# An attention loop's rounded copies of q and k: made by VectorE behind each pair's second reciprocal instead of by ScalarE

## The chip, the cores and the metric

One core of one Trainium2 chip runs the whole program in one launch. The metric is the device time of that launch in microseconds (us); lower is better.

## What is computed

The reference is a two-layer block over 16 sequences of 256 tokens with 256 features: a gated folding layer, then an attention layer with a mixture of eight experts behind it. The change is in the attention:

```python
h = _ln(x, ln1_g, ln1_b) + shift
qkv = (h @ Wqkv.T).reshape(b, n, 3, H, HD)               # H = 16 heads of HD = 64
q = _ln(qkv[:, :, 0].transpose(0, 2, 1, 3), qn_g, qn_b)
k = _ln(qkv[:, :, 1].transpose(0, 2, 1, 3), kn_g, kn_b)
scores = jnp.einsum('bhnd,bhmd->bhnm', q, k) / jnp.sqrt(jnp.float32(HD))
attn = jax.nn.softmax(scores, axis=-1)
o = jnp.einsum('bhnm,bhmd->bhnd', attn, v)
```

Matrix products that need float32 accuracy are made of three products of rounded parts. An operand `x` is split into `x_h`, its value rounded to the matmul's fp32r type, and `x_l = x - x_h`; the product is `x_h*y_h + x_h*y_l + x_l*y_h`.

## The kernel before

`attention` runs a software pipeline over batches. Step `t` works on eight pairs of heads, `s` = 0 to 7, of batch `t`, while it prepares batches `t+1` to `t+3` and finishes `t-1`. Each engine has its own instruction list, written out by hand in program order; semaphores tie them together. An engine that waits holds up all that stands behind in its list.

In one pair, TensorE makes the scores of two heads (L1107), then transposes the probabilities of the pair before (L1119), then does filling work: transposes of prepared q and k (`fill`, L1200), blocks of the qkv projection (`chunk`, with L147 as the line of its matmuls), the output projection, and in every second pair the products with v (L1134). The softmax of the pair goes VectorE `lowest_of` (L1493, row minima), ScalarE `exps` (L1262), VectorE `invert` (L1499, one reciprocal for each head, sides 0 and 1), GpSimd `divide` (L1392, one for each head), and back to TensorE's transposes in the next pair.

Beside this the q and k of batch `t+1` are prepared in eight blocks j of 128 x 512. A chunk of the projection lands in one of two PSUM banks. ScalarE copies it out (L1306) and squares it into `raw_sq` (L1308); only then is the bank free for the next chunk but one. VectorE sums the squares (`total`, L1489). ScalarE's square of chunk e waits for the sum of chunk e-2, because there are two `raw_sq` buffers:

```python
wait(act, summed, 8, b, e - 1)
nc.scalar.activation(raw_sq[e % 2][:, :], chunk_bank[j % 2][:, :], ACT.Square).then_inc(chunk_out, 1)
```

TensorE waits for that bank in `chunk` with `wait(pe, chunk_out, 12, b, j - 1)`. GpSimd scales the block (`norm`, L1380), TensorE transposes it (L1200), ScalarE puts the affine part on it (`empty`, L1286, which also frees the one transpose bank), ScalarE makes the rounded high part (`high_parts`, L1321), and GpSimd makes the low part (`low_parts`, L1386). In the first step, `t` = -1, VectorE makes the low parts (L1553). The places in the lists are:

```python
HIGH_PAIR = [3, 4, 5, 5, 6, 6, 7, 7]
LOW_PLACE = [(3,1),(4,1),(5,1),(5,1),(6,1),(6,1),(7,1),(7,1)]
CHUNK_PAIRS = [6, 6, 7, 7, 0, 0, 1, 1, 4, 4, 5, 5]
```

So the pairs 5, 6 and 7 hold two high parts each, and 3 and 4 hold one. GpSimd's list in such a pair is: divide side 0, divide side 1, low parts. In pair 5 a low part of the layer's input (`a_l`, L1418) stands between them; it waits for VectorE's `a_h` (L1547). In pair 6 the tiny power op for `rstd` (L1406) stands ahead of the divides, and VectorE's two normalizing ops (L1462) wait for it. VectorE's list in pair 7 is: the minima, `o_l` (L1512), reciprocal 0, the copy of `pT` (L1524), two statistics, a total, reciprocal 1 (L1499), two aggregates (L1475), the variance `out_var` (L1478, 128 x 2 elements), the second total (L1489), and then the minima of the next step's pair 0 (L1493). Step 14 is a little different: block 7 is emptied late in pair 7, and its high part stands behind that.

Of the kernel before, what the change touches and what calls it, by code (L numbers as in the profile page):

```python
# [20 lines left out]
ACT = mybir.ActivationFunctionType  # L21
# [3 lines left out]
NB, T, D = 16, 256, 256  # L25
# [15 lines left out]
def live(b):  # L41

    return not isinstance(b, int) or 0 <= b < NB


def wait(eng, sem, per, b, n):


    if n <= 0:
        b, n = b - 1, n + per  # L50
    if live(b):
        eng.wait_ge(sem, b * per + n)
# [814 lines left out]
HIGH_PAIR = [3, 4, 5, 5, 6, 6, 7, 7]  # L867
# [56 lines left out]
def fill_at(t, i):  # L924

    if i < 0:
        t, i = t - 1, i + 2 * PAIRS
    for name, j, slot in TR_FILLS:
        if slot == LATE_FILL and t == LAST_NEAR[0]:
            slot += 1  # L930
        if slot == i:
            return t + TR_LAG[name], name, j
    return -1, None, 0


def attention(nc, exponent, weights, rows_of, banks, ident, x1_rows, hbias, cols, x2_rows, logit, out, a, halves, sbuf, sems):
# [3 lines left out]
    x1_in, spread_in, spread_out, normed_x, tr_h, out_h, a_hi, a_lo, x1_out = norm_sems  # L940
    s = ExitStack()
    with s:
# [11 lines left out]
        qT_h, qT_l, kT_h, kT_l = (sbuf(s, n, [P, 12, T], F32R) for n in ("qT_h", "qT_l", "kT_h", "kT_l"))  # L954
# [31 lines left out]
        def closing(b):  # L986

            return isinstance(b, int) and b == NB - 1
# [19 lines left out]
        def o_part(o, q, its, n):  # L1008

            return o[:, o_at(q, its):o_at(q, its) + n, :].rearrange("p k t -> p (k t)")  # L1010
# [8 lines left out]
        def block_of(parts, j, its):  # L1019

            e = QK_ORDER[j]
            part = parts[e % QKC // 2]
            at = 4 + 4 * its if e % 2 else 0
            return part[:, at:at + 4, e // QKC * P:(e // QKC + 1) * P]

        def raw_block(j):

            return raw[:, QK_ORDER[j], :].rearrange("p (m n) -> p m n", m=4)
# [23 lines left out]
        with nc.Block() as block:  # L1052
# [202 lines left out]
            def _(act):  # L1255
# [17 lines left out]
                def empty(b, name, j, its):  # L1273
                    if name is None or not live(b) or name == "h" and first(b):
                        return
                    if name == "h":
                        wait(act, tr_h, 1, b, 1)
                        wait(act, a_lo, 1, b - 1, 1)
                        for k in range(KT):
                            last = nc.scalar.activation(aT[:, k, :], tr[:, k * T:(k + 1) * T], ACT.Identity,  # L1280
                                                        bias=hbias[:, k, bass.ds(b, 1)], scale=cols[:, LN1_G + k:LN1_G + k + 1])
                        last.then_inc(out_h, 1)
                    if name == "qk":
                        wait(act, tr_qk, 8, b, j + 1)
                        g = QN_G if QK_ORDER[j] % QKC < 2 else KN_G
                        nc.scalar.activation(raw_block(j), tr[:, :].rearrange("p (m n) -> p m n", m=4), ACT.Identity,  # L1286
                                             bias=cols[:, g + 1:g + 2], scale=cols[:, g:g + 1]).then_inc(out_qk, 1)
                    if name == "x2":
                        wait(act, tr_x2, 1, b, 1)
                        nc.scalar.activation(x2T[:, :, :].rearrange("p k n -> p (k n)"), fill_bank(b)[:, :], ACT.Copy).then_inc(out_x2, 1)  # L1290
                    if name == "gates":
                        wait(act, tr_gates, 1, b, 1)
                        nc.scalar.activation(logit[:, bass.ds(b * TT, TT), :], fill_bank(b)[:, 0:TT * E].rearrange("p (n e) -> p n e", n=TT), ACT.Copy).then_inc(out_gates, 1)

                def projected(b, n):
                    wait(act, tr_proj, TT, b, n + 1)
                    wait(act, tr_gates, 1, b - 1, 1)
                    nc.scalar.activation(proj[:, n, :], proj_bank(b, n)[:, 0:D], ACT.Copy).then_inc(out_proj, 1)
# [13 lines left out]
                            act.wait_ge(wo_lo, FIRST_LO + 4)  # L1312
                        nc.scalar.activation(v[1 - odd][:, n, (c - QKC) * 512:(c - QKC + 1) * 512], chunk_bank[j % 2][:, :], ACT.Copy).then_inc(chunk_out, 1)

                def high_parts(t, s, js, odd):
                    for j in js:
                        if live(t + 1) and HIGH_PAIR[j] == s:
                            if t == -1 and j == 0:
                                act.wait_ge(x1_out, 16 * NB)
                            wait(act, out_qk, 8, t + 1, j + 1)  # L1320
                            nc.scalar.activation(block_of((qT_h, kT_h), j, 1 - odd), raw_block(j), ACT.Copy).then_inc(qk_hi, 1)  # L1321

                def step(t, odd):
                    for s in range(PAIRS):
                        if not closing(t) and not closing(t - 1):
                            if s - 1 in PROJ_PAIRS and live(t - 1):
                                projected(t - 1, PROJ_PAIRS.index(s - 1))
                            empty(*fill_at(t, 2 * s - 1), 1 - odd)
                        for b, q, its, n in taken_at(t, s, odd):
                            if live(b):  # L1330
                                wait(act, pv_done, PAIRS, b, q + n)
                                if q in (0, 2):
                                    wait(act, tr_proj, TT, b - (2 if q == 0 else 1), TT)
                                nc.scalar.activation(o_part(o_h, q, its, n), result_of(b, q, n), ACT.Copy).then_inc(o_hi, n)
                        if closing(t) or closing(t - 1):
                            empty(*fill_at(t, 2 * s - 1), 1 - odd)
                        for n in range(TT):
                            if live(t + 1) and s == SEED_PAIR[n]:
                                seeds(t + 1, n)
                        late = t == LAST_NEAR[0] and s == PAIRS - 1  # L1340
                        if live(t):
                            exps(t, s, (0,))
                        if not late:
                            empty(*fill_at(t, 2 * s), 1 - odd)
                        if live(t):
                            exps(t, s, (1,))
                        b, q, _ = pair_at(t, s, 1, odd)
                        if live(b):
                            wait(act, pT_done, H, b, 2 * q + 1)
                            wait(act, pv_done, PAIRS, b, q - 1)  # L1350
                            nc.scalar.activation(pT[q % 2 * 2][:, :, :].rearrange("p m n -> p (m n)"), pT_bank[0][:, :], ACT.Copy).then_inc(pT_act, 1)  # L1351
                        high_parts(t, s, range(7 if late else 8), odd)
                        if late:
                            empty(*fill_at(t, 2 * s), 1 - odd)
                            high_parts(t, s, (7,), odd)
                        for c, j in chunks_at(t, s):
                            if live(c):
                                chunk(c, j, odd)
                        if closing(t) and s in PROJ_PAIRS:
                            projected(t - 1, PROJ_PAIRS.index(s))  # L1360
                        for q in range(4):
                            if t == -1 and s == WOUT_HIGH_PAIR[q]:
                                nc.scalar.activation(flat(wo_h[:, :, :])[:, q * 512:(q + 1) * 512], flat(o_raw)[:, q * 512:(q + 1) * 512], ACT.Copy).then_inc(wo_hi, 1)
                        if live(t) and s == PIECE_PAIRS[0]:
                            wait(act, ew_piece, 32, t, 16)
                            wait(act, ew_stored, 32, t - 1, 32)
                            nc.scalar.activation(ew_h[:, :], ew_raw[:, :], ACT.Copy).then_inc(ew_piece, 8)
# [57 lines left out]
            def _(dve):  # L1425
# [69 lines left out]
                def invert(t, s, side):  # L1495
                    at = s % 2 * 2 + side
                    wait(dve, exped, H, t, 2 * s + side + 1)
                    wait(dve, shared, H, t, 2 * s + side - 3)
                    nc.vector.reciprocal(share[:, at, :], denom[:, at, :]).then_inc(inverted, 1)  # L1499

                def step(t, odd):
                    far = t + 2
                    for s in range(PAIRS):
# [29 lines left out]
                            link.settle()  # L1533
                        if live(t):
                            invert(t, s, 1)
                        if s == OUT_STATS_PAIR:
                            for part in range(TT + 1, 2 * TT + 2):
                                out_norm(t, s, part)
# [600 lines left out]
```

## Time and profile before

| | |
|---|---|
| median of 3 runs | 1431.31 us (1430.86 to 1431.76) |
| the profiled execution | 1430.09 us, of which the span is 1428.3 us |
| busy: PE, ACT, DVE, POOL | 96%, 73%, 67%, 64% of the span |
| mean granted TensorE clock | 0.987 |

The profile has a page of the whole run, groups of instructions by line, waits, a timeline of single instructions for any stretch and busy time by window. PE is TensorE, ACT ScalarE, DVE VectorE, POOL GpSimd. A time such as 663.20 is us from the start of the span. The steps of the attention loop lie between about 326 and 1155 us, and the steps 2 to 13 repeat each other with a period of 50.8 us. Most rows below are from the end of step 5 and the start of step 6, whose pair 0 begins at 662.80.

### The profile page before, as it was taken

How to read it: one execution, taken by the hardware profiler on the slowest of the kernel's cores; microseconds unless marked ns; L12 is line 12 of the kernel's file. 1: busy time of each engine (PE TensorE's matmuls, PEld its weight loads, DVE VectorE, ACT ScalarE, POOL GpSimd, SP SyncE). 2: the span in 40 equal slices, each digit the busy share in tenths (PEclk: the TensorE clock that was granted, in tenths of full speed). 3: DMA queues.
4: the chain of work that ended last, by engine and by line, in shares of the span. 5: the costliest groups of instructions: out<-in, count | busy, mean ns of one | idle time of the engine just before them, and what ended most of it. 6: DMA issues, size and time to landing. Idle time of an engine off the chain costs nothing. (4 is left out here: it accounts for less than half of the span.)

```text
span 1428.3 us, 30431 instructions
## 1 busy us (share of the span) xinstructions
PE 1370.0 (96%) x10795; PEld 1184.1 (83%) x10795; DVE 960.9 (67%) x2191; ACT 1035.7 (73%) x2703; POOL 912.5 (64%) x855
## 2 busy tenths in 40 slices
PE   7899999997999999999999999999999988999996
PEld 6799999996688887887888888788888678889896
DVE  6876677654776676676667667667756568678763
ACT  5566666565898889889889888988988732476662
POOL 2576666652678768867877876886777620354643
PEclk9899999999999999999999999999999999999999
DMA  5342222110100100110110010011011046145522
GB/s 159 122 122 67 68 68 69 50 51 23 38 9 31 53 23 31 53 45 9 53 46 31 31 53 28 26 53 45 9 45 46 31 143 258 45 104 155 138 34 30
DMA packets 61638, 89.04 MB, mean 62 GB/s; under 512 B 6144, under 2 KB 50992, under 8 KB 58800
## 3 DMA queue, kind: packets, MB, share of 16 engines
q1 hardware_dynamic: 53232, 75.82, 16.4%
q0 software_dynamic: 6144, 8.39, 3.6%
q10 hardware_dynamic: 2112, 2.88, 0.6%
q8 instruction: 87, 1.43, 0.4%
q14 instruction: 63, 0.52, 0.1%
HBM read 61.90 MB, written 25.18 MB: 61 GB/s over the span
## 5 line engine op out<-in xcount | busy, mean ns | idle before, releaser
L1392 POOL TENSOR_TENSOR prob<-prob,share_p 128x512 f32<-128x512 f32 x256 | 271.6, 1067 | 196.1 <-DVE share_p L1499 195.6
L1493 DVE TENSOR_REDUCE shift<-bank 128x2 f32<-128x512 f32 x256 | 164.7, 685 | 185.9 <-PE bank L1107 185.8
L1262 ACT ACTIVATE prob<-bank,shift 128x256 f32<-128x256 f32 x512 | 237.8, 479 | 63.9 <-DVE shift L1493 63.8
L147 PE MATMUL bank<-wqkv_h,rowsT_h 128*128 128x512 f32 x384 | 159.3, 415 | 2.0 <-PEq L311 1.7
L147 PE MATMUL bank<-wqkv_h,rowsT_l 128*128 128x512 f32 x384 | 151.7, 395 | 0.0
L147 PE MATMUL bank<-wqkv_l,rowsT_h 128*128 128x512 f32 x384 | 151.3, 394 | 0.0
L1119 PE MATMUL bank<-ident,prob 128*128 128x128 f32 x1024 | 143.0, 281 | 1.3 <-POOL prob L1392 1.3
L1380 POOL TENSOR_TENSOR landing<-landing,rq 128x512 f32<-128x512 f32 x128 | 131.1, 1046 | 10.1 <-DVE rq L1447 10.1
L1134 PE MATMUL bank<-pT,landing 128*64 128x256 f32 x1024 | 126.2, 386 | 1.7 <-ACT pT L1351 1.7
L1119 PEld LDWEIGHTS bank<-ident,prob 128*128 128x128 f32 x1024 | 109.6, 141 | 21.7 <-POOL prob L1392 4.2
L1262 ACT ACTIVATION_READ_ACCUMULATOR prob<-bank,shift 128x1 f32 x512 | 107.3, 210 | 0.0
L1286 ACT ACTIVATE landing<-bank,cols 128x512 f32<-128x512 f32 x128 | 101.9, 796 | 5.8 <-PE bank L1200 4.2
L644 POOL TENSOR_TENSOR hid_l<-hid,hid_h 128x512 fp32r<-128x512 f32 x64 | 86.3, 1358 | 30.6 <-ACT hid_h L540 29.9
L536 ACT ACTIVATE hid<-bank,cols 128x256 f32<-128x256 f32 x128 | 53.3, 470 | 68.1 <-PE bank L147 67.9
L1134 PEld LDWEIGHTS bank<-pT,landing 128*64 128x64 f32 x1024 | 67.3, 137 | 40.8 <-issue 9.2
L1107 PE MATMUL bank<-kT_h,qT_h 64*128 64x256 f32 x512 | 85.6, 330 | 3.1 <-ACT prob L1262 3.1
L1489 DVE TENSOR_REDUCE ssq<-raw_sq 128x8 f32<-128x512 f32 x128 | 85.8, 672 | 3.2 <-ACT raw_sq L1308 2.6
L1524 DVE COPY pT<-bank 128x512 f32<-128x512 f32 x128 | 87.1, 681 | 0.4 <-PE bank L1119 0.4
L1306 ACT ACTIVATE landing<-bank 128x512 f32<-128x512 f32 x128 | 80.0, 625 | 9.1 <-PE bank L147 9.0
L1200 PE MATMUL bank<-ident,landing 128*128 128x128 f32 x512 | 78.4, 276 | 8.2 <-ACT landing L1286 3.7
L147 PEld LDWEIGHTS bank<-wqkv_h,rowsT_h 128*128 128x128 f32 x384 | 73.2, 191 | 15.5 <-issue 2.4
L147 PEld LDWEIGHTS bank<-wqkv_h,rowsT_l 128*128 128x128 f32 x384 | 72.7, 189 | 15.7
(324 smaller groups left out, 4518.3 us busy)
## 6 DMA issues: line engine op xcount, KB each, us to landing
landing<-in_fc1s SPq DMA_DIRECT2D x6, 1024.0 KB, 4.9
landing<-in_fc2s SPq DMA_DIRECT2D x6, 1024.0 KB, 5.1
rows<-in_x SPq DMA_DIRECT2D x16, 256.0 KB, 2.9
xT<-in_xT SPq DMA_DIRECT2D x16, 256.0 KB, 2.7
x_again<-in_x SPq DMA_DIRECT2D x16, 256.0 KB, 2.8
x_rows<-x SPq DMA_DIRECT2D x16, 256.0 KB, 3.2
rows<-x_rows SPq DMA_DIRECT2D x16, 256.0 KB, 3.1
x<-x_rows SPq DMA_DIRECT2D x16, 256.0 KB, 2.9
```

What stands on the lines that cost most here:

```text
L147: last = nc.tensor.matmul(out, a, b, start=(n == 0), stop=(n == 3 * len(ks) - 1))
L644: nc.gpsimd.tensor_tensor(hid_l[:, 2 * g:2 * g + 2, :], hid[:, 2 * g:2 * g + 2, :], hid_h[:, 2 * g:2 * g + 2, :].bitcast(F32), ALU.subtrac ...
L1107: mm = nc.tensor.matmul(score_bank[side][:, n * T:(n + 1) * T], q[r, at, n * P:(n + 1) * P], k[r, at, :], start=(i == 0), stop=(i == 2))
L1119: last = nc.tensor.transpose(pT_bank[side][:, m * T + n * P:m * T + (n + 1) * P], prob[q % 2 * 2 + side][:, n, m * P:(m + 1) * P], ident[: ...
L1134: last = nc.tensor.matmul(values_bank(b, q)[side * HD:(side + 1) * HD, :], v[its][:, m, h * HD:(h + 1) * HD], pT[q % 2 * 2 + side][:, m, : ...
L1262: last = nc.scalar.activation(prob[at][:, n, :], score_bank[side][:, n * T:(n + 1) * T], ACT.Exp, bias=shift[:, at, n:n + 1], scale=-1.0, ...
L1286: nc.scalar.activation(raw_block(j), tr[:, :].rearrange("p (m n) -> p m n", m=4), ACT.Identity, bias=cols[:, g + 1:g + 2], scale=cols[:, g ...
L1380: nc.gpsimd.tensor_tensor(part, part, rq[:, n, c * 8:(c + 1) * 8].unsqueeze(2).to_broadcast([P, 8, HD]), ALU.mult).then_inc(normed, 1)
L1392: nc.gpsimd.tensor_tensor(prob[at][:, :, :], prob[at][:, :, :], share[:, at, :].unsqueeze(2).to_broadcast([P, TT, T]), ALU.mult).then_inc( ...
L1489: nc.vector.tensor_reduce(ssq[:, n, c * 8:(c + 1) * 8], raw_sq[c % 2][:, :].rearrange("p (h d) -> p h d", h=8), AX, ALU.add).then_inc(summ ...
L1493: nc.vector.tensor_reduce(shift[:, s % 2 * 2 + side, :], score_bank[side][:, :].rearrange("p (n m) -> p n m", n=TT), AX, ALU.min).then_inc ...
L1524: nc.vector.tensor_copy(pT[q % 2 * 2 + 1][:, :, :].rearrange("p m n -> p (m n)"), pT_bank[1][:, :]).then_inc(pT_dve, 1)
```

## The change

The eight high parts of a step leave ScalarE's list. VectorE makes them with `tensor_copy`, in the same pairs, directly behind reciprocal 1 of the pair and ahead of whatever stood there. The semaphore `qk_hi` that the low parts wait for now counts VectorE's copies. Nothing else is moved.

```diff
 # scalar
-                def high_parts(t, s, js, odd):
-                    for j in js:
-                        if live(t + 1) and HIGH_PAIR[j] == s:
-                            if t == -1 and j == 0:
-                                act.wait_ge(x1_out, 16 * NB)
-                            wait(act, out_qk, 8, t + 1, j + 1)
-                            nc.scalar.activation(block_of((qT_h, kT_h), j, 1 - odd), raw_block(j), ACT.Copy).then_inc(qk_hi, 1)
...
-                        high_parts(t, s, range(7 if late else 8), odd)
                         if late:
                             empty(*fill_at(t, 2 * s), 1 - odd)
-                            high_parts(t, s, (7,), odd)
...
 # vector
+                def high_parts(t, s, odd):
+                    for j in range(8):
+                        if live(t + 1) and HIGH_PAIR[j] == s:
+                            if t == -1 and j == 0:
+                                dve.wait_ge(x1_out, 16 * NB)
+                            wait(dve, out_qk, 8, t + 1, j + 1)
+                            nc.vector.tensor_copy(block_of((qT_h, kT_h), j, 1 - odd), raw_block(j)).then_inc(qk_hi, 1)
...
                         if live(t):
                             invert(t, s, 1)
+                        high_parts(t, s, odd)
                         if s == OUT_STATS_PAIR:
                             for part in range(TT + 1, 2 * TT + 2):
                                 out_norm(t, s, part)
```

## Rows read from the trace of the kernel before

**Rows 1.** The page: the span, and each engine's busy time.

```profile
span 1428.3 us, 30431 instructions
PE 1370.0 (96%) x10795; PEld 1184.1 (83%) x10795; DVE 960.9 (67%) x2191; ACT 1035.7 (73%) x2703; POOL 912.5 (64%) x855
```

**Rows 2.** Windows, one steady step: length, then busy time and count by engine.

```profile
561.20:612.00 50.80, 50.70 (x394) 41.52 (x394) 34.56 (x77) 44.43 (x124) 38.73 (x36) 1.00 0.12 38
```

**Rows 3.** One line's instructions, L1321: ns min/median/max, first and last start.

```profile
L1321 ACT ACTIVATE qT_h<-landing x64: 612/648/657, 342.4 to 1117.0; 128x512 fp32r<-128x512 f32 x64
```

**Rows 4.** The same for the lines L1547 and L1478 of DVE.

```profile
L1547 DVE CAST rowsT_h<-rowsT x15: 414/415/643, 355.6 to 1056.3; 128x512 fp32r<-128x512 f32 x15
...
L1478 DVE TENSOR_SCALAR out_var<-out_moment x16: 168/962/968, 460.1 to 1163.6; 128x2 f32<-128x2 f32 x16
```

**Rows 5.** Timeline, DVE, end of pair 7: start, us, instruction, [idle before].

```profile
662.97 0.15 DVE L1499 RECIPROCAL share_p<-denom 128x2 f32<-128x2 f32 x1
663.04 0.23 DVE L1475 BATCH_NORM_AGGREGATE out_moment<-out_stats 128x2 f32<-128x6 f32 x2
663.30 0.96 DVE L1478 TENSOR_SCALAR out_var<-out_moment 128x2 f32<-128x2 f32 x1
664.18 0.67 DVE L1489 TENSOR_REDUCE ssq<-raw_sq 128x8 f32<-128x512 f32 x1
664.77 1.27 DVE L1493 TENSOR_REDUCE shift<-bank 128x2 f32<-128x512 f32 x2
```

**Rows 6.** Timeline, POOL, the same stretch.

```profile
663.20 1.04 POOL L1392 TENSOR_TENSOR prob<-prob,share_p 128x512 f32<-128x512 f32 x1 [1.00 <-DVE share_p L1499]
664.20 1.29 POOL L1386 TENSOR_TENSOR qT_l<-landing,qT_h 128x512 fp32r<-128x512 f32 x1
```

**Rows 7.** Timeline, ACT, the same stretch: the square of chunk e = 3.

```profile
664.89 0.60 ACT L1308 ACTIVATE raw_sq<-bank 128x512 f32<-128x512 f32 x1
```

**Rows 8.** Timeline, PE: first matmul of pair 0's second chunk.

```profile
666.16 0.39 PE L147 MATMUL bank<-wqkv_h,rowsT_h 128*128 128x512 f32 x1
```

**Rows 9.** Timeline, DVE and POOL, two casts elsewhere that meet POOL.

```profile
55.81 1.42 DVE L703 CAST rowsT_h<-rowsT 128x512 fp32r<-128x512 f32 x1
...
304.71 0.43 DVE L703 CAST h_h<-hT 128x512 fp32r<-128x512 f32 x1
...
55.67 1.28 POOL L689 TENSOR_TENSOR xT_l<-xT,xT_h 128x512 fp32r<-128x512 f32 x1
56.90 1.48 POOL L644 TENSOR_TENSOR hid_l<-hid,hid_h 128x512 fp32r<-128x512 f32 x1
...
304.77 1.51 POOL L672 TENSOR_TENSOR x_b<-x_again,ffn_b 128x512 f32<-128x512 f32 x1
```

**Rows 10.** Timeline, ACT from pair 5 to 6, and PE's fill of pair 6.

```profile
649.49 1.17 ACT L1321 ACTIVATE kT_h<-landing 128x512 fp32r<-128x512 f32 x2
...
651.48 0.82 ACT L1286 ACTIVATE landing<-bank,cols 128x512 f32<-128x512 f32 x1
...
651.86 0.49 PE L1119 MATMUL bank<-ident,prob 128*128 128x128 f32 x3
652.45 0.30 PE L1200 MATMUL bank<-ident,landing 128*128 128x128 f32 x1
```

**Rows 11.** Timeline, DVE and POOL, pair 6 and the start of 7.

```profile
655.40 2.17 DVE L1462 TENSOR_SCALAR rows<-rows,moment,rstd 128x256 f32<-128x256 f32 x2 [0.40 <-POOL rstd L1406]
659.12 0.69 DVE L1493 TENSOR_REDUCE shift<-bank 128x2 f32<-128x512 f32 x1 [1.55 <-PE bank L1107]
...
655.33 2.09 POOL L1392 TENSOR_TENSOR prob<-prob,share_p 128x512 f32<-128x512 f32 x2
```

**Rows 12.** Timeline, step 15: DVE's minima of pair 0, PE's scores of pair 1.

```profile
1118.42 1.28 DVE L1493 TENSOR_REDUCE shift<-bank 128x2 f32<-128x512 f32 x2
...
1121.11 0.39 PE L1107 MATMUL bank<-kT_h,qT_h 64*128 64x256 f32 x2 [0.32 <-ACT prob L1262]
```

**Rows 13.** Timeline, DVE, the first minima of step 0.

```profile
365.04 1.28 DVE L1493 TENSOR_REDUCE shift<-bank 128x2 f32<-128x512 f32 x2
```

## The prediction

> **What bounds the kernel now.** I read the page first, then one steady step by windows, then single instructions on all four engines around the places of the change. The page shows TensorE (PE) busy for 96% of the span, ScalarE 73%, VectorE 67% [rows 1]. One steady step shows it more sharply: PE is busy 50.70 of 50.80 us, ScalarE 44.43, VectorE 34.56 [rows 2]. So ScalarE has 6 us to spare per step and VectorE 16 us; neither sum sets the time. What ScalarE gives back is worth only what PE waits for it, and what VectorE gets costs nothing unless it makes a PE instruction late. The question is therefore one of order: which PE instruction stands close behind the places where VectorE now does more.
>
> **What is removed from ScalarE.** Per step eight activations of 0.65 us [rows 3], 5.2 us, 16 times over. Where does PE wait for ScalarE? In a steady step I find one place. In pair 5 two high parts run from 649.49 for 1.17 us, the chunk copies follow, then the `empty` that frees the transpose bank, 651.48 to 652.30. PE's next fill starts at 652.45, so 0.15 us is the delay from a ScalarE end to a PE start. The last of the three transposes ahead of it starts at about 652.08 (0.11 us between such starts), so the fill begins 0.37 us behind it where 0.11 would do [rows 10]. Without the two high parts `empty` is ready well before; the gain is 0.26 us per step. I count 13 steps: -3.4 us.
>
> **What VectorE gets.** Eight copies of 128 x 512. The same form, `a_h`, takes 0.415 us at the median (0.414 to 0.643) [rows 4]: 3.3 us per step, which the 16 us would hold. But these copies do not run alone. `out_var` on 128 x 2 elements takes 0.168 us at its shortest and 0.962 at the median [rows 4]. In the timeline it starts at 663.30, just behind POOL's divide (663.20, 1.04 us), and ends at 664.26, with the divide [rows 5, 6]. It was blocked for the whole POOL instruction. A cast elsewhere does the same: issued 0.14 us behind a POOL start it takes 1.42 us and ends 0.28 us behind POOL's end (57.23 against 56.95), and the next POOL instruction takes 1.48 us where its neighbour takes 1.28. A cast issued 0.06 us ahead of a POOL start keeps its 0.43 us and POOL takes 1.51, 0.23 longer, which is the 0.37 us of overlap less 0.14 [rows 9].
>
> The Trainium skill has a rule for this (SBUF — State Buffer, Who interferes with whom): a VectorE instruction that uses both of its SBUF ports, as fp32 copies and scalar ops between SBUF tensors do, and a GpSimd instruction exclude each other, and the one that issues first holds the pair to its end. The rows agree on the blocking (0.962 against 0.168 us); the skill gives no price for the 0.20 us of the next GpSimd instruction. By the rule the copies are the wrong work to put just where GpSimd's divide starts. Without the rule the sum would be -3.4 us.
>
> **Pair 7, step by step.** Reciprocal 1 starts at 662.97 and the next VectorE instruction at 663.04; the divide it releases starts at 663.20 [rows 5, 6]. So:
> - Cast of block 6: starts 663.05, 0.15 ahead of the divide, wins, ends 663.47. The divide loses 0.27 - 0.14 = 0.13 and ends at 664.37 instead of 664.24.
> - Cast of block 7: issued 663.39 with the divide under way, blocked, ends 664.37 + 0.28 = 664.65.
> - POOL's low part of block 6 needs only the first cast. It starts at 664.33 and takes 1.29 [rows 6] + 0.20 = 1.49, to 665.82.
> - The two aggregates follow the second cast by the old distances, and `out_var` is issued at 664.83, 0.26 behind the first aggregate [rows 5]. POOL is again busy: it ends at 665.83.
> - The second total started at 664.18, now 665.75: 1.57 us late. ScalarE's square of chunk 3 started 0.71 behind that total's start (664.89) and took 0.60 [rows 7]: now 666.46 to 667.06.
> - PE's second chunk of pair 0 needs that bank. It started at 666.16 [rows 8]; the bank was free at 665.49, with 0.15 of delay 665.64, so the slack is 0.52. Now the earliest start is 667.06 + 0.15 = 667.21: PE waits 1.05 us.
>
> The minima of pair 0 come 1.57 us late as well (664.77 before [rows 5]), and with them exps, reciprocals and divides. Pair 0 has room for that: the next scores move back by the same 1.05 us. I count nothing more. This holds for steps 1 to 13, which have both `out_var` and a chunk 3: 13 x 1.05 = +13.7 us.
>
> **The other pairs.** In pairs 3 and 4 one cast is added; pair 3's moves the weight-piece subtraction behind the divide, pair 4's waits for a divide. Both find PE busy with chunks or the projection. In pair 5 the two casts make `a_h`, and behind it `a_l` and two low parts, some 0.8 us late; their readers are in a later pair. In pair 6 the two casts come ahead of the two normalizing ops, which today take 2.17 us because each waits out a divide [rows 11]. VectorE then has four such instructions in a row, each let in at the end of one POOL instruction (a low part, the power op, two divides). The divides move back about 1.1 us, so they end near 658.6 and VectorE is free at 658.7. The minima of pair 7 are due at 659.12, or 658.86 if the 0.26 of pair 6 is gained, and VectorE idles 1.55 us ahead of them today [rows 11]. It fits, barely: cost nothing. If it does not, what is late next is the whole of pair 7.
>
> **The ends.** Step 14 has no chunk 3, but its pair 7 holds both casts and `out_var`. By the same working the minima of step 15 come about 1.6 us late (1118.42 before), and PE's scores of pair 1, which already waited 0.32 us for exps [rows 12], come 1.6 us late: +1.6. In step -1 VectorE now makes high and low parts in turn, so the first minima (365.04 [rows 13]) come some 0.5 us late and the scores of the next pair follow; against it I put 0.2 for ScalarE's relief there: +0.3.
>
> **Sum.** -3.4 + 13.7 + 1.6 + 0.3 = +12.2 us. Against the profiled execution (1430.09 us, span 1428.3) that is 1442.3; the median of the runs is 1.2 us above that execution, so 1431.31 + 12.2 = 1443.5 us. The cost is borne by one wait. If each of its parts is off by 0.3 us (the boundary of one POOL instruction is a step, not a slope), it is 13 x 0.3 = 4 us either way.
>
> **Rivals.**
> - *The POOL conflict costs PE nothing (faster).* The copies take 0.42 us each at plain price, in time that `out_var` spends waiting today (0.96 against 0.17 us). For it: VectorE has 16 us of room per step. The point that decides is the second total of pair 7: if it is late by less than 0.52 us, PE's chunk starts on time and only ScalarE's relief is left: -3.4 us, 1428 us. Against it: `out_var` would have to get in ahead of the low part, and [rows 9] show that a waiting cast takes that opening.
> - *Both casts get in ahead of the divide (slower, less).* The second is issued 0.08 us before the first one's end. Then the divide ends about 0.5 us late, PE's transposes of pair 7 wait for it, and `out_var` waits for the divide alone; the total is 0.6 late, about the slack. Per step +0.5 - 0.26, and +1 at the ends: +4, 1435 us. Against it: in [rows 9] a POOL instruction that is waiting starts as the blocker ends.
> - *Pair 6 overruns (slower, more).* If the last normalizing op misses the second divide's end, it waits for a low part of 1.29 us [rows 6], the minima of pair 7 are about 0.8 us late, and all of pair 7's chain with them: 13 x 0.8 = 10 more, 1453 us.
> - *Nothing to be seen (same).* The relief and a small stall balance: within 3 us.
>
> **Chances.** Forecast 0.62; the first rival 0.08; both casts ahead 0.11; pair 6 overruns 0.12; balance 0.07. About 0.2% (2.9 us) is what a measurement of this kernel can tell from no change. Slower 0.85, same 0.08, faster 0.07. The range takes in the smaller-loss rival and nearly the overrun: 1435 to 1452; the forecast's own is 1439 to 1448.
>
> **What would show it.** In the changed profile: no ScalarE copies of q and k; in pairs 5 to 7 one cast near 0.42 us and one near 1.3; `out_var` starting more than 1 us later and still near 1 us long; ScalarE's square of chunk 3 waiting about 1.5 us for the total; a PE wait of about 1 us in L147 for that square, once a step; a period of 51.6 us in place of 50.8; the 0.37 us ahead of pair 6's fill gone. A period of 50.5 would make the first rival right; a late first minimum in pair 7 the third.

## The result and the profile after

The changed kernel took 1446.58 us (median of 4 runs, 1445.95 to 1451.81) where the kernel before took 1431.53 us beside it. The ratio is 1.0116, with a 95% interval of 1.0102 to 1.0130: slower by 1.2%. The medians differ by 15.0 us; the forecast was +12.2 us and the range 1435 to 1452.

The profiled execution is the slowest of the four, 1451.81 us. Up to PE's scores of step 15, pair 1 (1137.85, against 1121.11 in [rows 12]) it is 16.74 us behind the one before. The other 5.0 us come after that, where the records of granted clock show two half-clock stretches of 10.2 us (from 1139.4 and 1183.8) and before one of 3.4 us (from 1165.9). The other three runs are 5 to 6 us shorter at a granted clock of 0.988 to 0.989 (0.982 here), so I count those 5.0 us to that execution and not to the change.

Page: the span and each engine's busy time.

```profile
span 1450.0 us, 30432 instructions
PE 1381.2 (95%) x10795; PEld 1188.1 (82%) x10795; DVE 1046.5 (72%) x2319; ACT 974.2 (67%) x2575; POOL 926.6 (64%) x855
```

Exactly 128 instructions went from ACT to DVE; DVE's busy time rose by 85.6 us, ACT's fell by 61.5 [rows 1]. 128 plain casts of 0.415 us are 53 us: the other 32 us are, by the rows below, instructions that are counted as busy while they are blocked.

Windows, one steady step from pair 0 to pair 0, to be set beside [rows 2]: length, busy time and count of PE, PEld, DVE, ACT and POOL, then clock, DMA share and GB/s.

```profile
615.46:667.46 52.00, 51.09 (x394) 41.47 (x393) 39.79 (x85) 40.59 (x115) 39.61 (x36) 1.00 0.11 37
```

The period is 52.00 us in place of 50.77 to 50.81, and PE now has 0.91 us of idle time in it, where it had 0.10, with the same 394 matmuls to do. Its busy time is 0.39 us longer all the same, so part of what it loses stands as busy time in this view. What it waits for is in the view of waits (total us, times, longest); the first row below was not there before, and the second stood at 0.3 us once.

```profile
PE bank L147 <- ACT raw_sq L1308: 8.2, 13, 0.6
...
PE bank L147 <- issue: 3.8, 14, 0.5
```

The first is the wait that was forecast, 13 times. The view has only the 0.62 us between the modelled end of one matmul and the start of the next; the pair is 1.03 us longer. Timeline of pair 7's end (pair 0 of step 6 begins at 667.46), DVE, then POOL, ACT and PE; the rows answer to [rows 5 to 8].

```profile
667.62 0.15 DVE L1489 RECIPROCAL share_p<-denom 128x2 f32<-128x2 f32 x1
667.70 0.41 DVE L1497 CAST qT_h<-landing 128x512 fp32r<-128x512 f32 x1
668.02 1.26 DVE L1497 CAST kT_h<-landing 128x512 fp32r<-128x512 f32 x1
669.20 0.23 DVE L1465 BATCH_NORM_AGGREGATE out_moment<-out_stats 128x2 f32<-128x6 f32 x2
669.47 0.98 DVE L1468 TENSOR_SCALAR out_var<-out_moment 128x2 f32<-128x2 f32 x1
670.37 0.67 DVE L1479 TENSOR_REDUCE ssq<-raw_sq 128x8 f32<-128x512 f32 x1
...
667.86 1.14 POOL L1382 TENSOR_TENSOR prob<-prob,share_p 128x512 f32<-128x512 f32 x1 [1.01 <-DVE share_p L1489]
668.96 1.47 POOL L1376 TENSOR_TENSOR qT_l<-landing,qT_h 128x512 fp32r<-128x512 f32 x1
...
671.08 0.60 ACT L1308 ACTIVATE raw_sq<-bank 128x512 f32<-128x512 f32 x1 [2.25 <-DVE ssq L1479]
...
670.70 0.40 PE L147 MATMUL bank<-wqkv_h,rowsT_l 128*128 128x512 f32 x1
671.73 0.50 PE L147 MATMUL bank<-wqkv_h,rowsT_h 128*128 128x512 f32 x1 [0.62 <-ACT raw_sq L1308]
```

Read it downwards. The divide starts at 667.86, 0.16 behind the first cast, and ends at 669.00. The second cast, free to go at 668.02, ends at 669.28, 0.28 behind the divide. By then the low part is running (668.96 to 670.43), and `out_var`, 128 x 2 elements, stands for 0.98 us until that too is over. So the second total starts 2.91 us behind the start of pair 0, where it stood at 1.38 [rows 5]; the square of chunk 3 ends at 671.68 and PE's chunk starts 0.05 behind that end, 4.27 us behind the start of pair 0 in place of 3.36 [rows 8]. Pair 0 is 8.16 us long in place of 7.13.

The second wait, "issue", is not in the forecast. Timeline of pair 5's end and pair 6's start (654.84), DVE, POOL and PE.

```profile
653.71 0.17 DVE L1489 RECIPROCAL share_p<-denom 128x2 f32<-128x2 f32 x1 [0.20 <-DVE stats L1442]
653.79 1.59 DVE L1497 CAST kT_h<-landing 128x512 fp32r<-128x512 f32 x2
...
655.65 0.43 DVE L1546 CAST rowsT_h<-rowsT 128x512 fp32r<-128x512 f32 x1
...
656.16 1.26 POOL L1408 TENSOR_TENSOR rowsT_l<-rowsT,rowsT_h 128x512 fp32r<-128x512 f32 x1 [1.06 <-DVE rowsT_h L1546]
...
656.67 0.60 PE L1200 MATMUL bank<-ident,landing 128*128 128x128 f32 x4
657.52 0.47 PE L147 MATMUL bank<-wqkv_h,rowsT_h 128*128 128x512 f32 x1 [0.25 <-issue]
```

The fill (656.67) now follows the transposes without a gap, as forecast. But `a_h` is made behind the two casts, `a_l` (named `rowsT_l` here) ends at 657.42, and PE's next chunk starts 0.10 behind it. The code says why:

```python
if j == 0:
    wait(pe, a_hi, 1, b, 1)
    wait(pe, a_lo, 1, b, 1)
```

Chunk 0 stands in pair 6. Before, `a_l` ended 1.87 us behind pair 6's start and the chunk began 2.48 behind it; now these are 2.58 and 2.68. Pair 6 is 7.92 us long, where it was 7.72 to 7.76 and should have become 7.5.

### The profile page after: what moved, and what is told of

Read it like the earlier page. It is cut to its first block and busy times, and to the rows that moved or that the text cites. A ratio compares the mean times of both kernels' runs of the same rounds, so it can differ in the third digit from the quotient of the medians.

```text
span 1450.0 us, 30432 instructions
## 1 busy us (share of the span) xinstructions
PE 1381.2 (95%) x10795; PEld 1188.1 (82%) x10795; DVE 1046.5 (72%) x2319; ACT 974.2 (67%) x2575; POOL 926.6 (64%) x855
## 5 line engine op out<-in xcount | busy, mean ns | idle before, releaser
L147 PE MATMUL bank<-wqkv_h,rowsT_h 128*128 128x512 f32 x384 | 160.3, 417 | 13.7 <-ACT raw_sq L1308 8.2
L147 PE MATMUL bank<-wqkv_h,rowsT_l 128*128 128x512 f32 x384 | 151.9, 396 | 0.0
L147 PE MATMUL bank<-wqkv_l,rowsT_h 128*128 128x512 f32 x384 | 151.2, 394 | 0.0
L1308 ACT ACTIVATE raw_sq<-bank 128x512 f32<-128x512 f32 x128 | 80.3, 627 | 34.6 <-DVE ssq L1479 34.6
L147 PEld LDWEIGHTS bank<-wqkv_h,rowsT_h 128*128 128x128 f32 x384 | 72.8, 190 | 34.9 <-ACT raw_sq L1308 14.3
L1376 POOL TENSOR_TENSOR qT_l<-landing,qT_h 128x512 fp32r<-128x512 f32 x60 | 86.9, 1448 | 0.0
```

The source lines that it names most:

```text
L147: last = nc.tensor.matmul(out, a, b, start=(n == 0), stop=(n == 3 * len(ks) - 1))
L1376: nc.gpsimd.tensor_tensor(block_of((qT_l, kT_l), j, 1 - odd), raw_block(j), block_of((qT_h, kT_h), j, 1 - odd).bitcast(F32), ALU.subtract) ...
```

## The experiments

All of them are timed against the kernel before, in two groups: total_first to behind_a_h (median of before 1432.27 us) and pair5_only to reduce_copy (1430.56). The ratio is the one on record for runs taken side by side, not the quotient of the two medians. "Pair 0", "pair 6" and "pair 7" are the times from one pair's scores to the next pair's in a steady step.

| run | median us | ratio (95%) | period | pair 0 | pair 6 | pair 7 |
|---|---|---|---|---|---|---|
| before (profile) | 1431.53 | 1 | 50.8 | 7.13 | 7.72 | 4.70 |
| after (profile) | 1446.58 | 1.0116 (1.0102 to 1.0130) | 52.0 | 8.16 | 7.92 | 4.69 |
| total_first | 1435.07 | 1.0026 (1.0016 to 1.0037) | 51.1 | 7.23 | 7.94 | 4.70 |
| tiny_copies | 1427.84 | 0.9972 (0.9959 to 0.9984) | 50.55 | 7.16 | 7.47 | 4.70 |
| pair7_only | 1448.85 | 1.0108 (1.0091 to 1.0125) | 52.0 | 8.16 | 7.92 | 4.69 |
| behind_a_h | 1464.94 | 1.0227 (1.0210 to 1.0244) | 53.35 | 9.04 | 7.47 | 5.61 |
| pair5_only | 1440.40 | 1.0073 (1.0059 to 1.0086) | 51.5 | 8.01 | 7.47 | 4.82 |
| end_of_pair | 1426.64 | 0.9971 (0.9961 to 0.9981) | 50.5 | 7.13 | 7.47 | 4.70 |
| block7_tiny | 1443.77 | 1.0093 (1.0078 to 1.0109) | 51.9 | 7.98 | 7.95 | 4.70 |
| reduce_copy | 1439.79 | 1.0069 (1.0053 to 1.0085) | 51.4 | 7.88 | 7.62 | 4.70 |

**1. The second total ahead of `out_var`.** If PE waits for the square because `out_var` holds the total up, changing their order takes the wait away and leaves both casts where they are.

```diff
                         if s == OUT_STATS_PAIR:
-                            for part in range(TT + 1, 2 * TT + 2):
+                            for part in range(TT + 1, 2 * TT + 1):
                                 out_norm(t, s, part)
...
                         if before:
                             total(*before[1])
+                        if s == OUT_STATS_PAIR:
+                            out_norm(t, s, 2 * TT + 1)
```

> The changed kernel with one thing reordered on VectorE in pair 7: out_var stands behind the second total instead of ahead of it; both casts stay behind reciprocal 1. Theory (the loss of pair 0 comes from out_var waiting out a GpSimd low part with the total behind it): the total is late by the two casts and one divide only, about 0.6 us, against a slack of 0.5, so PE's wait for the square of chunk 3 shrinks from 1.04 to about 0.1 us a step; 13 steps give about -12 us against the changed kernel, +4 to +5 us (+0.3%) against the kernel before. Rival (VectorE is simply late by the casts' own time, wherever out_var stands): no more than 0.2 us a step comes back, +13 us or more against the kernel before.

The ratio fell from 1.0116 to 1.0026, and the wait for `raw_sq` left the list of waits. Its timeline, DVE and ACT (pair 0 begins at 663.10):

```profile
663.65 1.26 DVE L1497 CAST kT_h<-landing 128x512 fp32r<-128x512 f32 x1
...
665.00 0.65 DVE L1479 TENSOR_REDUCE ssq<-raw_sq 128x8 f32<-128x512 f32 x1
665.57 0.52 DVE L1468 TENSOR_SCALAR out_var<-out_moment 128x2 f32<-128x2 f32 x1
...
665.68 0.60 ACT L1308 ACTIVATE raw_sq<-bank 128x512 f32<-128x512 f32 x1 [1.22 <-DVE ssq L1479]
```

The second cast is as long as before, 1.26 us, yet the total comes 1.90 us behind pair 0's start in place of 2.91. The two casts alone make it 0.52 late (1.38 before), which is the slack that the forecast gave the chunk. The 0.1 us that pair 0 still loses is not that wait: side 1's divide, 1.14 us in place of 1.04, brings the transposes of pair 7's side 1 0.10 us late (1.59 us behind pair 0's start in place of 1.49). The other microsecond is `out_var` behind the low part. Of the 0.3 us of period that are left, 0.2 are pair 6.

**2. Tiny copies.** The same instructions, on 2 of each head's 128 columns from step 1 on; most of the high parts is left out.

```diff
-nc.vector.tensor_copy(block_of((qT_h, kT_h), j, 1 - odd), raw_block(j)).then_inc(qk_hi, 1)
+n = P if t < 1 else 2
+nc.vector.tensor_copy(block_of((qT_h, kT_h), j, 1 - odd)[:, :, 0:n], raw_block(j)[:, :, 0:n]).then_inc(qk_hi, 1)
```

> The changed kernel, but from step 1 on each of VectorE's copies covers only 2 of every 128 columns (128 x 8 elements in place of 128 x 512), so the high parts are mostly stale there; instruction count and order are unchanged. Theory (blocking by the GpSimd instruction under way, not the copies' length): the second cast and out_var each still wait out a GpSimd instruction, the second total is still about 1.2 us late, PE still waits about 0.7 us a step, and the kernel stays some 8 us (+0.5%) above the kernel before. Rival (the copies' own 0.42 us each are the cost): the loss goes, and with ScalarE's relief the time is 3 us under the kernel before.

What I expected failed: nothing was blocked that had not been before. DVE, then POOL:

```profile
661.21 0.15 DVE L1498 CAST qT_h<-landing 128x8 fp32r<-128x8 f32 x1
661.27 0.17 DVE L1498 CAST kT_h<-landing 128x8 fp32r<-128x8 f32 x1
...
661.37 1.04 POOL L1382 TENSOR_TENSOR prob<-prob,share_p 128x512 f32<-128x512 f32 x1 [1.00 <-DVE share_p L1489]
```

Two such casts start 0.06 us apart and both start ahead of the divide. So this was no test of the blocking. It bounds the other side: with VectorE's part nearly free, the kernel is 0.28% faster (0.16 to 0.41%), which agrees with the -3.4 us (0.24%) of the forecast's first term for ScalarE's relief.

**3. Only block 7's copy tiny.** This leaves the first cast at full length, so that the second meets a divide under way (most of block 7's high part is left out).

```diff
+n = P if t < 1 or j < 7 else 2
```

> The changed kernel, but from step 1 on the copy of block 7 alone covers 2 of every 128 columns, so that block's high part is mostly stale; block 6 in front of it is copied in full, as are all others. This mends the run with all copies tiny, where both were through before the divide began. Theory (blocking): block 7's tiny copy is issued under the divide, waits it out and takes about 1.0 us in place of 0.15, out_var then waits out the low part, the second total is 1.3 to 1.4 us late and pair 0 still takes about 8.0 us: +13 to +15 us against the kernel before. Rival (the copies' length): 0.4 us of VectorE time are gone, the total is late by no more than block 6's 0.35 us, pair 0 takes 7.1 to 7.2 us, +3 us or less against the kernel before.

DVE, then POOL:

```profile
665.36 0.41 DVE L1498 CAST qT_h<-landing 128x512 fp32r<-128x512 f32 x1
665.68 1.00 DVE L1498 CAST kT_h<-landing 128x8 fp32r<-128x8 f32 x1
...
666.87 1.06 DVE L1468 TENSOR_SCALAR out_var<-out_moment 128x2 f32<-128x2 f32 x1
...
665.52 1.14 POOL L1382 TENSOR_TENSOR prob<-prob,share_p 128x512 f32<-128x512 f32 x1 [1.01 <-DVE share_p L1489]
666.62 1.28 POOL L1376 TENSOR_TENSOR qT_l<-landing,qT_h 128x512 fp32r<-128x512 f32 x1
```

A cast of 128 x 8 elements takes 1.00 us here and 0.17 us in experiment 2. It costs nearly what the full one does: pair 0 is 7.98 us, 0.85 of the 1.03 us lost, and the kernel 13.2 us slower, as expected. It is the place of the second copy that is paid for, its size hardly.

**4. The same copies by an operation that is not blocked.** `tensor_reduce` with the maximum over one element copies too.

```diff
-nc.vector.tensor_copy(block_of((qT_h, kT_h), j, 1 - odd), raw_block(j)).then_inc(qk_hi, 1)
+nc.vector.tensor_reduce(block_of((qT_h, kT_h), j, 1 - odd), raw_block(j).unsqueeze(3), AX, ALU.max).then_inc(qk_hi, 1)
```

> The changed kernel with each copy made by a tensor_reduce over one element (a maximum), at the same places; it takes about 0.67 us in place of 0.41, like the other reductions of this size, which were never seen to be blocked. Theory: neither copy is blocked and GpSimd is not slowed (its low parts back to 1.29 us), but out_var still falls behind the low part of block 6 and waits it out; the total is about 1.2 us late, pair 0 takes 7.8 us, pair 6 about 7.7: +8 to +11 us against the kernel before. Rival (the casts' own conflict with GpSimd is the whole of the loss): within 3 us of the kernel before.

DVE, then POOL:

```profile
666.03 0.68 DVE L1497 TENSOR_REDUCE kT_h<-landing 128x512 fp32r<-128x512 f32 x1
666.62 0.24 DVE L1465 BATCH_NORM_AGGREGATE out_moment<-out_stats 128x2 f32<-128x6 f32 x2
666.89 1.03 DVE L1468 TENSOR_SCALAR out_var<-out_moment 128x2 f32<-128x2 f32 x1
...
665.61 1.04 POOL L1382 TENSOR_TENSOR prob<-prob,share_p 128x512 f32<-128x512 f32 x1 [1.00 <-DVE share_p L1489]
666.60 1.29 POOL L1376 TENSOR_TENSOR qT_l<-landing,qT_h 128x512 fp32r<-128x512 f32 x1
```

The copy runs through under the divide in 0.68 us, and the divide and the low part keep their 1.04 and 1.29 us. The Trainium skill says the same of `tensor_reduce` (SBUF — State Buffer, Who interferes with whom): on trn2 it never contends with GpSimd; the trace agrees, 0.68 us beside a divide and 0.67 elsewhere. Yet the pair still loses 0.75 us: `out_var` (666.89) comes 0.29 us behind the start of the low part (666.60). So the loss needs no blocked cast; any delay that brings `out_var` behind that start is enough. It does not follow that blocking is harmless in the changed kernel. These copies start 0.59 us apart, where plain casts that find GpSimd idle start 0.33 apart (experiment 8). By that estimate two plain casts that were not blocked would put `out_var` at about 666.37, 0.23 ahead of the low part. No run here has such casts; if the estimate is right, it is the blocking of the second cast that makes the delay long enough.

**5. Part of the change: pair 7 alone.** Blocks 0 to 5 stay on ScalarE, 6 and 7 go to VectorE. So that `qk_hi` counts in order, each copy waits for the one before it.

```diff
+ON_ACT, ON_DVE = (0, 1, 2, 3, 4, 5), (6, 7)
...
 # scalar, in its old place
+wait(act, qk_hi, 8, t + 1, j)
...
 # vector, behind reciprocal 1
+wait(dve, qk_hi, 8, t + 1, j)
```

> The kernel before with only blocks 6 and 7 (pair 7) given to VectorE behind reciprocal 1; blocks 0 to 5 stay on ScalarE, with a wait that keeps the count of high parts in order. Theory (pair 7 alone carries the loss of pair 0): pair 0 takes 8.17 us in place of 7.13 as in the changed kernel, 13 x 1.04 = +13.5, and +2 at the two ends: about +15 us (+1.0 to +1.1%) against the kernel before, with pair 6 at its old 7.72. Rival (the loss needs the backlog of all pairs): +8 us or less.

Pair 0 is 8.16 us, exactly that of the full change: pair 7's two copies make the whole of this loss. Pair 6 did not keep its old 7.72. Timeline of ACT in pair 5:

```profile
654.57 1.39 ACT L1323 ACTIVATE kT_h<-landing 128x512 fp32r<-128x512 f32 x2
```

It is 0.22 us longer than the same two in [rows 10]: with the added wait the second no longer overlaps the first. The `empty` behind them, and with it the fill of pair 6, come about 0.2 us later. That is my edit and not the change, and the ratio of this run (1.0108) says nothing of pair 6.

**6. Pair 5's copies behind `a_h`.** If `a_l` is what holds the chunk of pair 6 up, this brings pair 6 down to 7.5.

```diff
-                        high_parts(t, s, odd)
+                        if s != SPLIT_PAIR:
+                            high_parts(t, s, odd)
...
                             nc.vector.tensor_copy(a_h[:, :, :], aT[:, :, :]).then_inc(a_hi, 1)
+                        if s == SPLIT_PAIR:
+                            high_parts(t, s, odd)
```

> The changed kernel with the two casts of pair 5 moved behind a_h. Theory (pair 6 lost 0.20 us instead of gaining 0.26 because a_h and with it GpSimd's a_l came late, and PE's first chunk of pair 6 waits for a_l): a_h is on time, pair 6 takes 7.46 in place of 7.92 us, and 12 steps give -5.5 us against the changed kernel, so about +11 us (+0.8%) against the kernel before; pair 0 keeps its 8.17. Rival (pair 6 is late for another reason, such as VectorE's late minima there): no change against the changed kernel, or slower, because the minima of pair 6 come still later.

Pair 6 came down to 7.47 us, and the waits of L147 put down to "issue" went with it. But the kernel is 2.3% slower than before, where 0.8% was expected. DVE, from pair 5 to pair 7, then PE:

```profile
660.63 1.83 DVE L1497 CAST kT_h<-landing 128x512 fp32r<-128x512 f32 x2
662.38 1.28 DVE L1483 TENSOR_REDUCE shift<-bank 128x2 f32<-128x512 f32 x2
...
665.81 0.99 DVE L1497 CAST qT_h<-landing 128x512 fp32r<-128x512 f32 x1
666.72 1.26 DVE L1497 CAST kT_h<-landing 128x512 fp32r<-128x512 f32 x1
667.90 2.67 DVE L1452 TENSOR_SCALAR rows<-rows,moment,rstd 128x256 f32<-128x256 f32 x2
670.49 1.28 DVE L1483 TENSOR_REDUCE shift<-bank 128x2 f32<-128x512 f32 x2
...
673.28 0.39 PE L1107 MATMUL bank<-kT_h,qT_h 64*128 64x256 f32 x2 [0.85 <-ACT prob L1262]
...
675.75 0.66 PE L1119 MATMUL bank<-ident,prob 128*128 128x128 f32 x4 [0.91 <-POOL prob L1382]
```

Now the minima of pair 6 are the late ones: 2.18 us behind its start, where they stood at 1.15 in the changed kernel. Its four blocked instructions then stand at 665.81 to 670.57, one POOL instruction after the other, and the minima of pair 7 follow at once (670.49). This is the overrun of the third rival. The changed kernel is clear of it by the 0.82 us that DVE idles ahead of those minima:

```profile
663.77 1.29 DVE L1483 TENSOR_REDUCE shift<-bank 128x2 f32<-128x512 f32 x2 [0.82 <-PE bank L1107]
```

A shift of about a microsecond uses them up, and pair 7 (5.61) and pair 0 (9.04) pay.

**7. Pair 5's copies alone, behind `a_h`,** the other six on ScalarE, with the same added wait as in experiment 5 (`ON_DVE = (2, 3)`).

> The kernel before with only blocks 2 and 3 (pair 5) given to VectorE, behind a_h; the other six stay on ScalarE, with waits that keep the count of high parts in order. Theory: ScalarE's relief in pair 5 ends PE's wait at pair 6's fill (7.46 to 7.50 us for pair 6 in place of 7.74), a_h is on time, and the late minima of pair 6 (about 1 us, as in the run with the casts behind a_h) cost nothing because VectorE has only the two normalizing ops to do in pair 6 and can catch up before pair 7: -2.5 to -3.5 us (-0.2%) against the kernel before. Rival: the late minima of pair 6 already make pair 7 late, and the time is 5 us or more above the kernel before.

The ratio is 1.0073: the rival's time came, but not by its way. ACT, then PE:

```profile
660.85 0.61 ACT L1309 ACTIVATE raw_sq<-bank 128x512 f32<-128x512 f32 x1
...
662.47 0.51 ACT L1263 ACTIVATE prob<-bank,shift 128x256 f32<-128x256 f32 x1
...
666.96 0.66 PE L1120 MATMUL bank<-ident,prob 128*128 128x128 f32 x4 [0.81 <-POOL prob L1394]
```

Pair 6 has its 7.47, but its minima start late. The minima of pair 7 are on time again (1.01 us behind its start, as before the change); it is ScalarE that does not catch up. It works without a gap from pair 6's exponentials to those of pair 7 (662.47), which start 2.70 us behind the pair's start in place of 1.74, and these and their divide are late for PE. The added wait on ScalarE can account for little of these 0.96 us directly: in pair 6 its two high parts start 0.75 us apart in place of 0.53.

**8. All copies at the end of their pair.** The same eight copies, placed behind everything else in VectorE's list for the pair: behind `out_var` and the totals, behind `a_h`, behind the normalizing ops.

```diff
-                        high_parts(t, s, odd)
                         if s == OUT_STATS_PAIR:
...
                             chains(t, i + 1, spot)
+                        high_parts(t, s, odd)
```

> The changed kernel with all eight copies on VectorE, but at the end of the pair's list: behind the second total, a_h and the two normalizing ops. Theory (place, not work, made the loss): in pair 7 the total is on time, so pair 0 is back at 7.13 to 7.2; in pair 6 the normalizing ops are not queued behind casts, and the casts end before pair 7's minima are due, because GpSimd stands idle until it gets block 4; in pair 5 a_h is on time. ScalarE's relief remains: period 50.5 in place of 50.8, -2 to -4 us against the kernel before (ratio 0.998). Rival (16 us of idle VectorE time cannot be used at all, since some minima come late wherever the casts stand): 5 us or more above the kernel before.

1426.64 us over 9 runs, ratio 0.9971 to before (0.9961 to 0.9981): a small gain, clear of the noise, and faster than both kernels. Windows of one step, then DVE and POOL at the end of pair 7 (pair 0 begins at 659.91):

```profile
609.36:659.91 50.55, 50.55 (x395) 41.55 (x394) 39.47 (x85) 40.40 (x115) 39.51 (x36) 1.00 0.12 38
```

```profile
660.40 0.96 DVE L1468 TENSOR_SCALAR out_var<-out_moment 128x2 f32<-128x2 f32 x1
661.28 0.68 DVE L1479 TENSOR_REDUCE ssq<-raw_sq 128x8 f32<-128x512 f32 x1
661.88 0.41 DVE L1497 CAST qT_h<-landing 128x512 fp32r<-128x512 f32 x1
662.21 0.42 DVE L1497 CAST kT_h<-landing 128x512 fp32r<-128x512 f32 x1
662.54 1.28 DVE L1483 TENSOR_REDUCE shift<-bank 128x2 f32<-128x512 f32 x2
...
662.37 1.41 POOL L1376 TENSOR_TENSOR qT_l<-landing,qT_h 128x512 fp32r<-128x512 f32 x1 [1.03 <-DVE qT_h L1497]
```

PE is busy for the whole step. `out_var` still waits out the divide, as it did before the change, and the total is in its old place (1.37 us behind pair 0's start). Now POOL waits for the cast, and so both casts find it idle and take 0.41 and 0.42 us. The low part starts 2.46 us behind pair 0's start, where it stood at 1.40 [rows 6], and nobody misses it. DVE works as much as in the changed kernel (39.47 against 39.79 us): the same work costs 1.45 us of period less by its place alone.

## Why the prediction was right, and where it was not

The direction, the place and the size of the main term held.

- **Pair 7.** Each of these steps came within 0.1 us of the working: first cast ahead of the divide by 0.16 (0.15 forecast), second cast 0.28 behind the divide's end, low part 1.47 (1.49), total 2.91 behind the start of pair 0 (2.95), pair 0 longer by 1.03 (1.05), in the 13 pairs that were counted: 13.4 us (13.7). The last step has some luck in it: PE's chunk began 0.05 us behind the square and not 0.15, so it is 0.91 us late and not 1.05; but its second matmul follows the first after 0.33 us where it was 0.23, and that makes most of the rest. Experiment 1 shows `out_var` behind the low part to be the cause; experiments 3 and 4 show that a tiny but blocked second copy, or two slower ones that are not blocked, lead there too. That a change of order at one POOL boundary decides ("a step, not a slope") fits experiments 1 and 3; the delay at which the step lies was not tried.
- **ScalarE's relief.** The gain of 0.26 us per step was real: pair 6 is 7.47 in experiments 2, 6, 7 and 8.
- **The step that failed** is in pair 5: "a_h, and behind it a_l and two low parts, some 0.8 us late; their readers are in a later pair". Its size was about right (0.7 us), but the first reader of `a_l` is chunk 0 in pair 6, the very next pair. It takes the 0.26 back and 0.2 more, 12 times in steps 1 to 12: +2.5 us. In step 13 nothing stands between the casts and `a_h`, `a_l` ends 2.19 us behind the start of pair 6, and a gain is left (7.52 against 7.74); step 14 makes no `a_l` and has one too (5.88 against 6.00): together -0.35. The first term of the sum was -3.4 us and came out at +2.2. Experiment 6 shows the cause.
- **The ends.** Step 15, pair 0 is 5.87 in place of 4.36: +1.5 (+1.6 forecast). The first scores come 0.5 late, as forecast. In step 15, pair 1, the profiles of experiments 1, 3, 4 and 6 have 3.99 us where it was 4.47; the changed kernel's profile has 6.06 there, in a half-clock stretch, and cannot show whether it gets that 0.5 back. Step 0 is 0.8 us shorter in the profile after, where 0.2 was put, but that is the clock's doing: in the profile before it has a half-clock stretch at 384.2, in pair 4 (9.87 us), and none after (8.24), which is -1.6. That stretch comes and goes between the runs (pair 4 is 9.75 in experiment 4's profile). The other pairs of step 0 are 0.8 us longer (pair 0 by 0.5, pair 6 by 0.2), so apart from the clock the start costs about 1.3 us where the forecast had 0.3.
- **Pair 6 overruns.** "It fits, barely" held for the changed kernel, with 0.82 us left, but 0.46 of that is the length that pair 6 has beyond its 7.46; without it some 0.36 would be left (an estimate), where the forecast had 0.16. Its four instructions were not all held up as forecast: the first cast takes 0.77 us and the second 0.41 (659.42 and 660.12), beside the power op. Experiment 6 shows how near the overrun was.

The sum of the profile up to step 15, pair 1: 13.4 + 2.2 + 1.5 + 0.5 - 0.8 = 16.8 us, which are the 16.74 us by which it is behind. This is one profile cut into its parts and not a second measurement. The medians differ by 1.7 us less, and by 3.4 us less once the half-clock stretch of step 0 is taken out; that rest is not explained. The median came out 3.1 us above the forecast, and the 5.6 us by which pair 6 missed its term are more than that.

The rivals: no cost to PE, both casts ahead of the divide, and balance are ruled out by the rows of pair 7; the overrun did not come in this kernel.

## What to carry to other kernels

When a copy moves to VectorE, ask in which gap of GpSimd's list it falls, not only how long it takes. Here the same eight copies cost 15 us directly behind the instruction that releases GpSimd, and gained 4 behind VectorE's own urgent work, with GpSimd waiting for the copy. Moving only pair 5's two to a later place, behind `a_h`, made it worse: a loss of 33 us. The price is not paid by the copy alone but by the next short instruction that slips past the start of the following GpSimd instruction, and by whatever waits for that one. And of everything that stands behind a new instruction, look up the first reader in the code, in each list; "in a later pair" was true of `a_l` here, but the later pair was the next one, and that step cost the forecast most.

## What was not expected of the hardware

- Two casts of 128 x 8, 0.06 us apart, both start ahead of a divide that starts 0.16 us behind the first; with a first cast of 0.41 us the second is shut out and takes 1.00 us.
- GpSimd's first low part in pair 0, the one behind the two casts of pair 7, takes 1.46 us at the median of 13 steps of the changed kernel, and 1.29 before; behind the reductions of experiment 4 it takes 1.29, behind the tiny cast of experiment 3 1.28. What the longer duration consists of was not tried.
- A wait that the view puts down to "issue" was a semaphore of another engine: of PE's 3.8 us, 3.5 stand in 13 waits for `a_l`, one in pair 6 of each step from 0 to 12, and its end lies 0.10 us ahead of every one of these starts.
